# Rows for the experts and for attention passes 2 to 4 transposed by DMA instead of TensorE, in an attention and mixture-of-experts layer on eight cores

## The reference

```python
# layer norm -> gated linear attention (16 heads of 128) -> RMS norm -> Wo, residual
q = silu(x @ Wq.T); f = sigmoid(x @ Wk.T); log_f = log_sigmoid(f); v = x @ Wv.T
S_t = diag(f_t) S_{t-1} + outer(1 - f_t, v_t);  o_t = q_t @ S_t
x = x + rmsnorm(o) @ Wo.T
# layer norm -> top 2 of 8 experts (softmax gate) + one shared expert, residual
h = einsum('td,eid->eti', xf, w1)
g = silu(h) * einsum('td,eid->eti', xf, w3)
eo = einsum('eti,edi->etd', g, w2)
y = einsum('etd,te->td', eo, comb)             # comb: the two gate weights of a token
z = (silu(xf @ ws1.T) * (xf @ ws3.T)) @ ws2.T  # the shared expert
x = x + y + z
```

## Time and profile before

| | |
|---|---|
| median of 3 runs | 2378.13 us |
| the profiled execution | 2381.81 us |
| its span on the slowest core, core 4 | 2380.2 us |
| spans of the eight cores | 2364.4, 2348.0, 2372.2, 2371.5, 2380.2, 2377.7, 2357.6, 2379.1 us |
| TensorE busy | 2251.3 us, 95% |
| VectorE, ScalarE, GpSimd busy | 45%, 29%, 14% |
| mean granted TensorE clock, core 4 | 0.979 |
| the chain that ended last | TensorE 71%, DMA 14%, VectorE 8% |
| read from HBM and written | 577.84 MB and 109.05 MB |

### The profile page before, as it was taken

One profiled execution on the slowest core, in us unless ns is written; L12 is line 12 of the kernel. 1 busy time (PEld: TensorE's weight loads), 2 busy tenths in 40 slices (PEclk: granted clock), 3 DMA queues, 4 the chain that ended last, 5 costly groups with the idle time before them and its releaser, 6 DMA issues.

```text
span 2380.2 us, 44339 instructions; the slowest of 8 cores (2348.0 to 2380.2 us)
## 1 busy us (share of the span) xinstructions
PE 2251.3 (95%) x15680; PEld 1401.6 (59%) x15680; DVE 1066.1 (45%) x2174; ACT 700.0 (29%) x1346; POOL 331.9 (14%) x539
## 2 busy tenths in 40 slices
PE   5999998989998999999999999999999999998997
PEld 4666554556645655566444457767666586683443
DVE  6666665666655766565541231121121212211366
ACT  4444542355515553344321101121111212111000
POOL 1110110112101210111111011111101011011230
PEclk9999999999999999999999999999999999998998
DMA  7999976688838886698699689799999799999998
GB/s 124 198 191 220 197 136 162 184 160 151 148 137 186 158 139 131 185 205 139 131 259 222 153 243 180 160 191 191 242 193 194 149 186 202 185 222 185 245 317 286
DMA packets 110735, 445.55 MB, mean 187 GB/s; under 512 B 12416, under 2 KB 12432, under 8 KB 100368
## 3 DMA queue, kind: packets, MB, share of 16 engines
q0 software_dynamic: 76640, 278.47, 67.4%
q1 hardware_dynamic: 33840, 163.59, 19.6%
HBM read 577.84 MB, written 109.05 MB: 289 GB/s over the span
## 4 chain that ended last, share of the span: by engine, by line
PE 71%; DMA 14%; DVE 8%; issue 5%; ACT 1%; DVEq 0%; POOL 0%; SPq 0%; ACTq 0%; POOLq 0%
PE ps L773 14%; PE ps L732 12%; PE ps L448 11%; PE ps L742 9%; PE ps L461 8%; PE ps L422 6%; PE ps L433 6%; DMA wr<-w_t 3%; DVE FW L1120 3%; DMA out<-acc 2%; DMA eo<-eos 1%; PE ps L666 1%; DMA out<-y 1%; DVE Tt L1173 1%; DMA xp<-x_own 1%
## 5 line engine op out<-in xcount | busy, mean ns | idle before, releaser
L742 PE MATMUL ps<-xg,wr 128*128 128x256 bf16 (+2 forms) x2048 | 274.2, 287 | 5.0 <-issue 4.9
L773 PE MATMUL ps<-wr,gb 128*128 128x512 bf16 x1152 | 255.2, 384 | 7.4 <-DMA wr<-w_t 7.3
L433 PE MATMUL ps<-xT,wq 128*128 128x512 bf16 x1024 | 247.2, 385 | 8.6 <-ACT th L876 5.1
L1060 ACT ACTIVATE sil<-ps 128x256 bf16<-128x256 f32 (+2 forms) x160 | 74.8, 469 | 610.1 <-PE ps L732 477.9
L1603 POOL DMA_DIRECT2D wr<-w_t x240 | 128.1, 547 | 872.0 <-PE ps L742 385.7
L732 PE MATMUL ps<-xg,wr 128*128 128x256 bf16 x2048 | 244.7, 273 | 0.6 <-ACT eos L1080 0.4
L1445 DVE TENSOR_TENSOR gb<-sil,ps 128x256 bf16<-128x256 bf16 (+1 forms) x128 | 62.4, 488 | 407.5 <-PE ps L732 306.6
L448 PE MATMUL ps<-wv,xT 128*128 128x256 bf16 x2048 | 238.5, 276 | 5.2 <-DMA wv<-wv_t 2.1
L422 PE MATMUL ps<-xT,wk 128*128 128x512 bf16 x1024 | 233.7, 381 | 8.4 <-DMA wk<-wk_t 8.0
L461 PE MATMUL ps<-wo,ob 128*128 128x512 bf16 x1024 | 229.8, 383 | 6.4 <-DVE y L1295 3.7
L742 PEld LDWEIGHTS ps<-xg,wr 128*128 128x128 bf16 x2048 | 199.9, 98 | 55.3 <-issue 6.9
(11 more groups left out here) (159 smaller groups left out, 2559.6 us busy)
## 6 DMA issues: line engine op xcount, KB each, us to landing
wr<-w_t POOLq DMA_DIRECT2D x240, 512.0 KB, 29.5
wv<-wv_t POOLq DMA_DIRECT2D x64, 512.0 KB
wk<-wk_t POOLq DMA_DIRECT2D x64, 512.0 KB, 13.0
wq<-wq_t POOLq DMA_DIRECT2D x64, 512.0 KB, 12.0
xs<-x2T SPq DMA_DIRECT2D x40, 512.0 KB, 18.6
y1d<-y SPq DMA_DIRECT2D x20, 1024.0 KB, 5.5
xst<-xs SPq DMA_DIRECT2D x40, 512.0 KB, 19.1
eo<-eos SPq DMA_DIRECT2D x40, 512.0 KB, 9.2
```

The source lines that it names most:

```text
L433: ins = t.matmul(self.ps[:, b, :], self.wq[i % 2][:, k * 128:(k + 1) * 128], self.xT[q % 2][:, k, :], start=(k == 0), stop=(k == 15))
L742: ins = t.matmul(self.ps[:, bk, 0:w], self.wr[c % NRING][:, k * 128:(k + 1) * 128], self.xg[(b - 1) % 2][:, k, 256:256 + w], start=(k == 0 ...
L773: ins = t.matmul(self.ps[:, bk, :], lhs, self.wr[c % NRING][:, dg * 512:(dg + 1) * 512], start=(ic == 0), stop=(ic == 7))
L1060: a.activation(self.sil[n % 2][:, 0:w], self.ps[:, self.bank[0, b, ic, s], 0:w], AF.Silu).then_inc(self.a_sil, 1)
```

## The change

Five things are changed.

1. `pe_xg` is gone, with the copies out of PSUM on ScalarE and VectorE and the tiles `xst`. SyncE's queue loads the rows of an expert from `xs` straight into `xg`, transposed, by five DMAs (`sp_xg`). The first of them waits until the hidden products of the block that last read this place are done (for experts 0 and 1, those of block 0).
2. `pe_ln` is gone for passes 2 to 4, with ScalarE's copies. ScalarE's queue issues one transposing DMA from `xb` in SBUF to `xT` for each row tile (`act_xT`), at the heads where it copied before. The products of these passes wait on the DMAs' semaphore `d_ln`; GpSimd's load of the next `xb` waits on it too.
3. In passes 2 and 3 the norm stands at heads 3, 6, 9, 12, after the gates and ahead of the mask (the wait for TensorE's scores), and ScalarE's scale stands in the same step after its gates (`act_next`).
4. `WIDTHS` has four entries: 240, 272, 304, 384.
5. In SyncE's queue the loads of `acc` tiles 2 to 4 stand ahead of expert 0's rows, and the last four `s3x` loads are issued one block earlier.

```diff
-WIDTHS = (256, 304, CAP - 256)
+WIDTHS = (240, 272, 304, 384)
@@ pe_k, and the same in pe_v
-        t.wait_ge(self.a_ln, 2 * (ln_index(q, 3 if q else 2) + 1))
+        if q < 2:
+            t.wait_ge(self.a_ln, 2 * (ln_index(q, 3 if q else 2) + 1))
+        else:
+            t.wait_ge(self.d_ln, 64 * (q - 1))
@@ pe_program
-                if h in (2, 6, 10, 14):
-                    self.pe_ln(t, 2, h // 4, self.xb)
...
-            if h in (4, 7, 10, 13) and 1 < q < 4:
-                self.pe_ln(t, q + 1, (h - 4) // 3, self.xb)
@@ pe_ffn
-            if b < NX:
-                self.pe_xg(t, b)
@@ pe_hidden
-            t.wait_ge(self.a_xg, 5 * b)
-            t.wait_ge(self.v_xg, 5 * b)
...
+                    if 0 < b < NB - 1 and ic == 0 and wh == 0:
+                        for j in ((2, 3, 4) if s else (0, 1)):
+                            t.wait_ge(self.d_xg[j], 16 * b)
@@ new, called from act_program in place of act_ln
+    def act_xT(self, a, q, i):
+        a.wait_ge(self.v_xn1, ln_index(q, i) + 1)
+        a.dma_start(self.xT[q % 2][:, :, i * 128:(i + 1) * 128], self.xb[:, :],
+                    transpose=True).then_inc(self.d_ln, 16)
@@ new, called in act_program right after act_gates
+    def act_next(self, a, q, h):
+        if h in (3, 6, 9, 12) and 1 < q < 4:
+            self.act_rs1(a, ln_index(q + 1, h // 3 - 1))
@@ dve_program
-            if h in (4, 7, 10, 13) and 1 < q < 4:
-                self.dve_norm(v, ln_index(q + 1, (h - 4) // 3), self.xb)
...
                 self.dve_gates(v, g + 1)
+            if h in (3, 6, 9, 12) and 1 < q < 4:
+                self.dve_norm(v, ln_index(q + 1, h // 3 - 1), self.xb)
             self.dve_mask(v, g)
@@ pool_xb
-            p.wait_ge(self.t_ln, 2 * L)
+            p.wait_ge(self.d_ln, 16 * (L - 7))
@@ in place of sp_xst
+    def sp_xg(self, s, e, j):
...
+        if j == 0:
+            s.wait_ge(self.t_u3, HN[max(e - 1, 0), 7, 1])
         r = e * CAP + j * 128
+        s.dma_start(self.xg[e % 2][:, :, j * 128:(j + 1) * 128], self.xs[r:r + 128, :],
+                    transpose=True).then_inc(self.d_xg[j], 16)
```

More of the change, by code:

```diff
@@ L214, in __init__ @@
         self.xg = [at("xg%d" % i, [128, 16, CAP], BF16, 20480 * i) for i in range(2)]
-        self.xst = [at("xst%d" % i, [128, D], BF16, 40960 + 4096 * i) for i in range(5)]
         self.gb = at("gb", [128, 8, CAP], BF16, 77824)
@@ L263, in __init__ @@
         self.d_s3x = [sem("d_s3x%d" % i) for i in range(2)]
-        self.d_xst = [sem("d_xst%d" % i) for i in range(5)]
+        self.d_xg = [sem("d_xg%d" % i) for i in range(5)]
         self.d_eo = [sem("d_eo%d" % i) for i in range(2)]
@@ L441, in pe_v @@
         nt = 4 if q else 3
-        t.wait_ge(self.a_ln, 2 * (ln_index(q, nt - 1) + 1))
+        if q < 2:
+            t.wait_ge(self.a_ln, 2 * (ln_index(q, nt - 1) + 1))
+        else:
+            t.wait_ge(self.d_ln, 64 * (q - 1))
         b = self.take(t, ("v", n, a), (self.a_v, 2 * n + a + 1))
@@ L656, in pe_program @@
             self.pe_general(t)
-    def pe_xg(self, t, e):
-        for j in range(5):
-            n = 5 * e + j
-            t.wait_ge(self.d_xst[j], 16 * (e + 1))
-            for hf in range(2):
-                b = self.take8(t, ("xg", n, hf), (self.v_xg if hf else self.a_xg, n + 1))
-                for k in range(8):
-                    ins = t.transpose(self.pbf(b)[:, k * 128:(k + 1) * 128],
-                                      self.xst[j][:, (8 * hf + k) * 128:(8 * hf + k + 1) * 128],
-                                      self.iden[:, :])
-            ins.then_inc(self.t_xg, 1)
     def pe_ffn(self, t):
@@ L713, in pe_hidden @@
                         t.wait_ge(self.d_s3x[s], 64)
+                    if 0 < b < NB - 1 and ic == 0 and wh == 0:
+                        for j in ((2, 3, 4) if s else (0, 1)):
+                            t.wait_ge(self.d_xg[j], 16 * b)
                     bk = self.take8(t, (wh, b, ic, s), (self.v_g, n) if wh else (self.a_sil, n))
                     if s and 0 < b < NB - 1:
-                        with t.If(self.count > 256 + WIDTHS[0]):
-                            with t.If(self.count > 256 + WIDTHS[1]):
+                        with t.If(self.count > 256 + WIDTHS[1]):
+                            with t.If(self.count > 256 + WIDTHS[2]):
+                                self.pe_tail(t, b, c, wh, bk, WIDTHS[3])
+                            with t.Else():
                                 self.pe_tail(t, b, c, wh, bk, WIDTHS[2])
+                        with t.Else():
+                            with t.If(self.count > 256 + WIDTHS[0]):
+                                self.pe_tail(t, b, c, wh, bk, WIDTHS[1])
                             with t.Else():
-                                self.pe_tail(t, b, c, wh, bk, WIDTHS[1])
-                        with t.Else():
-                            self.pe_tail(t, b, c, wh, bk, WIDTHS[0])
+                                self.pe_tail(t, b, c, wh, bk, WIDTHS[0])
                         continue
@@ L1021, in act_program @@
                     self.act_gates(a, g + 1)
+                self.act_next(a, q, h)
                 if g > 31:
@@ L1032, in act_program @@
                 self.act_v(a, VAT[g][0], VAT[g][1], 0)
-            if h in (3, 6, 9, 12) and 1 < q < 4:
-                self.act_rs1(a, ln_index(q + 1, h // 3 - 1))
             if q >= 2 and h in (1, 4):
@@ L1065, in act_ffn @@
                     self.act_ex(a, 14 + ic)
-            if b < NX:
-                for j in range(5):
-                    n = 5 * b + j
-                    a.wait_ge(self.t_xg, n + 1)
-                    a.copy(self.xg[b % 2][:, 0:8, j * 128:(j + 1) * 128],
-                           self.pbf(self.bank["xg", n, 0]).rearrange("p (k t) -> p k t", t=128)
-                           ).then_inc(self.a_xg, 1)
             if 0 < b < NB - 1:
@@ L1456, in dve_ffn @@
                         self.dve_mix(v, T)
-            if b < NX:
-                for j in range(5):
-                    n = 5 * b + j
-                    v.wait_ge(self.t_xg, n + 1)
-                    v.tensor_copy(self.xg[b % 2][:, 8:16, j * 128:(j + 1) * 128],
-                                  self.pbf(self.bank["xg", n, 1]).rearrange("p (k t) -> p k t", t=128)
-                                  ).then_inc(self.v_xg, 1)
             if b == 0:
@@ L1749, in sp_xst @@
                 s.wait_ge(self.d_sc[i], 32 * len(range(i, 16, 3)))
-            s.wait_ge(self.t_wo, 64)
-        if e:
-            s.wait_ge(self.t_xg, 5 * (e - 1) + j + 1)
+        if j == 0:
+            s.wait_ge(self.t_u3, HN[max(e - 1, 0), 7, 1])
         r = e * CAP + j * 128
-        s.dma_start(self.xst[j][:, :], self.xs[r:r + 128, :]).then_inc(self.d_xst[j], 16)
+        s.dma_start(self.xg[e % 2][:, :, j * 128:(j + 1) * 128], self.xs[r:r + 128, :],
+                    transpose=True).then_inc(self.d_xg[j], 16)
     def sp_program(self, s):
@@ L1796, in sp_program @@
         self.sp_acc(s, 1)
-        for j in range(5):
-            self.sp_xst(s, 0, j)
         for a in range(2, 5):
             self.sp_acc(s, a)
+        for j in range(5):
+            self.sp_xg(s, 0, j)
         for a in range(8):
```

19 lines of the change are left out of this document (7 added, 12 removed).

## The result

The changed kernel takes 2544.56 us (median of 4 runs, 2523.58 to 2742.64) beside 2381.34 for the kernel before (4 runs): slower by a factor of 1.0656, interval 1.0573 to 1.074, some 156 us. Forecast were 2336 us, within 2300 to 2430. In some executions of any of these kernels the cores of one die run at a lower clock and take longer; ratios leave these out, and where a run's median holds such executions, the times of the others are given one by one.

A forecast was written before the change was run, and what follows sets the result against it. TensorE, busy 95% of the span, was taken as the bound, with DMA nearly full in the expert blocks. Attention -14.6 and experts -27.5 gave -42.1 against the median 2378.1, so 2336.0 us, range 2300 to 2430.

The forecast's parts named there:

- The bound: Whole kernel: TensorE, busy 95% of the span, bounds it; in the expert blocks DMA is nearly full too.
- a share of 1.05: Expert blocks: DMA share reached inside block 1 while weights are owed, taken as the DMA engines' ceiling.
- Experts, the transfer's price: Expert blocks: each transposed row tile takes 2.0 us of all 16 engines, 2.5 us more in blocks 2 to 7.
- The upper end: Expert row tiles: 24 us each, if each of 16 pieces took what a whole row takes.
- The slow-transfer rival: Expert blocks: at 5 us a tile experts take 54.7 us more, w2 tiles arrive late; 2417 us, chance 0.27.
- waits for weights above 10 us in each block: Expert blocks: sign that the forecast is wrong, named beside block 1 or 5 growing.
- Widths: Expert products: narrower columns spare core 4's TensorE 13 us, nearly all masked by waits for weights.
- Attention: Attention passes: -15.1 transposes, -1.9 copy wait, -7.0 norm waits, +9.4 stall, together -14.6 us.
- the third rival: Attention: at 17 us latency xb's load lands late, 8 + 25 us lost, 2369; chance 0.14, shared with 3-4 us transfers.
- The stall at head 14 of pass 1: Attention: TensorE waits 9.4 us (2.1 to 19.7) for pass 2's last transposed tile, at 8.8 us latency.
- the waits for the norm: Attention: of 14.0 us in which TensorE waited for the norm, half, 7.0, was taken as saved.
- the output copy behind the scale's table load: Attention, ScalarE: a 1.28 us table load ahead of the copy, 8 times; taken at 0, 10 us if on the path.

The follow-up runs named there:

- e8: Kernel before plus 18 DMAs on SyncE's queue after its last store, nothing else moving; a transposing load alone was issued in 2.1 us and landed in 4.5.
- e3: Kernel before with only the experts' rows transposed by DMA from SyncE's queue, three widths; 2437.93 us, ratio 1.0227.
- e15: Kernel before with two tails under one If, widths 304 and 384; ratio 0.9977 (0.9927 to 1.0027).
- e14: e2 with its transposing DMAs replaced by plain copies of whole 4096-byte rows, untransposed; 2395.08 and 2392.68 us beside 2389.55.
- e2: Kernel before with only attention passes 2 to 4 transposed by DMA from ScalarE's queue and the norm moved; 2446.46 us, ratio 1.0253.
- e4: Kernel before with only the norm and ScalarE's scale one step earlier, transposes kept on TensorE; 2382.85 us, ratio 1.0004.
- e5: e3 with each load of expert rows a plain copy in the same 256-byte pieces, not transposed; 2442.45 us beside 2403.34 for the kernel before.
- e6: e3 with the stores of eo issued by ScalarE and the transposes of expert 2 and later held back; 2576.98 us beside 2403.34 for the kernel before.
- e11: e5 with four of five row tiles of each expert loaded two at a time in 512-byte pieces; ratio to the kernel before 1.0013.
- e12: e2 with its 12 transposing DMAs issued by SyncE instead of ScalarE; 2426.29 and 2444.42 us beside 2381.42 for the kernel before.
- e9: Kernel before with its three widths, tails in a row under their own conditions instead of nested with Else; ratio 1.0022.

## Why the prediction was wrong

**The bound.** Right that TensorE was the bound, and that DMA stood close behind. Wrong in what "DMA" was taken to be: a sum of bytes over 16 engines. What ended the waits was a queue (SyncE's) and TensorE's supply of instructions, neither of which the sum had a term for. Nor was a share of 1.05 a ceiling: it is 1.14 from 1690 to 1789 us after the change, at 160 GB/s.

**Experts, the transfer's price: a failed step, 54 us.** "I take 2.0, near the lower end, because the bytes are the same and only the writes are cut up." Alone the tile costs 3.3 us, in the expert blocks beside the weights 18 to 20 in the mean (e8, the trace after). The upper end, 24 us from one row's time a piece, was the nearer. The slow-transfer rival had the sign, and that its 54.7 at 5 us a tile is so near e3's 54 is luck: the tile cost nearly four times that, and the mechanism was another. w2 tiles were not late on core 0; the queue was held for a block's length, and eo's stores, the copies into `eos` and TensorE's banks stood behind. Of the signs that the forecast named for it, "waits for weights above 10 us in each block" never came, but block 1 did grow, from 100.1 to 109.6 us on core 4, and every block to 8 is longer there, block 5 least (108.7 to 109.4).

**Widths: a failed step, 65 us.** "... the widths, 13 us on TensorE, are nearly all masked." The masking was not far off: e15 computes 19.8 us more columns on core 4 and loses nothing that can be measured. But the cost was sought in columns alone. The that gave the prices also had an idle column, 4.9 us of "issue" before the last-placed tail; it was never asked what a fourth tail adds to a program that is only just supplied in time.

**Attention: a failed step, 60 us instead of -14.6.** "I take 8.8, the row that also starts in SBUF ..." 8.9 is what a copy of whole rows takes (e14); in pieces it is 15.9 to 18.5 from ScalarE's queue (median of e2, and of the changed kernel on core 4). Two terms were missing: the issue, 8.5 us on ScalarE's queue, ahead of copies that TensorE needs; and its consequence on GpSimd, where the third rival (17 us, `xb` late, 2369) was right in mechanism and under half in size: 33 us where 75 came, since weights stood behind the load of `xb` as well. The stall at head 14 of pass 1, 9.4 forecast, was 5.7 on core 0 and 6.7 on core 4. Two smaller terms were off and cancel: the waits for the norm went whole, 14.0 us where 7.0 were taken, and the output copy behind the scale's table load, taken at 0 with 10 as its bound, cost 11.6 us (e4).

**The sum.** 65 + 60 + 54 = 179 by parts, 156 to 163 together; the parts share some waits. The chance of 0.30 for slower was small for three untried terms, each priced near its cheap end.

## What to carry to other kernels

Count the packets of a transfer, not only its bytes: here a tile that a DMA writes in 2048 pieces of 256 bytes cost little alone, and five in a row held the queue of the engine that issued them, with all that stood behind it, once the weights kept the DMA engines full. Count the instructions of a step too, those that a branch skips among them, against the time of the step; in this kernel, 5 us of "issue" idle time before one tail was the sign that there was no room for another. And price an unknown operation with the machine loaded as it will be: where bounds lie a factor of ten apart, the cheap end was here the idle machine's.

## What the runs showed of the hardware

- A DMA of 128 x 2048 in 256-byte pieces, transposing or not: landing 4.4 to 4.5 us alone (e8); five in a row beside the weights, 17 to 20 us of the queue each in the mean (e5, after), fifteen 21.5 (e6).
- A short issue can leave its cost to the next one: with room in block 0, a transposing load took 5.12 us and the store of a running sum behind it 0.53 (core 0, after); a plain one in the same pieces took 0.53 and the store behind it 4.65 (core 5, e5).
- Pieces of 512 bytes at the written end were not cut into packets of their own, pieces of 256 bytes were (e11: 2272 packets an expert, e5: 10240).
- TensorE was supplied with 34 to 35 instructions a us, loads and matmuls counted, in the steps with four and five tails; skipped ones count.
- The granted clock can fall at such a gap: on core 0 after the change, 16 products of 240 columns took 1.81 us at 1605.24 and 3.25 us at 1618.23, each behind 2.38 us of idle time. The granted clock was 1.00 in the first stretch and 0.53, near the lower of the two levels (1.2 and 2.4 GHz), in the second.

Not settled: why e6 is slower than e3, why one or two cores stay late in e12, whether fewer packets or fewer DMAs freed the queue in e11, and what sets the rate of instructions. No version that was run beats the kernel before; e9, e11, e15 and e4 tie with it, e14 comes within 0.2%, and the outputs of e11 and e14 are not the reference's.
